# A routed expert kernel: a table of the first 32 tiles, built in eleven pieces beside attention, and a re-ordered turn to the experts

## The reference

```python
x = x + tanh(g_xattn) * attention(layernorm(x), ctx, ctx)
z = layernorm(x)
logits = tanh(z @ Wg1.T) @ Wg2.T
top_logits, top_idx = top_k(logits, 2)
scores = zeros.at[rows, top_idx].set(softmax(top_logits))
up   = einsum('td,ehd->teh', z, Wup) + bup        # 8 experts, 256 wide
down = einsum('teh,eoh->teo', silu(up), Wdown) + bdown
x = x + tanh(g_ffn) * einsum('te,teo->to', scores, down)
```

## Time and profile before

| | us |
|---|---|
| profiled execution, whole | 730.69 |
| its span (first to last instruction) | 728.7 |
| median of three runs | 727.93 |
| PE busy | 639.2 (88%) |
| DVE busy | 520.3 (71%) |
| ACT busy | 381.5 (52%) |
| POOL busy | 356.5 (49%) |

### The profile page before, as it was taken

One profiled execution on the slowest core, in us unless ns is written; L12 is line 12 of the kernel. 1 busy time (PEld: TensorE's weight loads), 2 busy tenths in 40 slices (PEclk: granted clock), 3 DMA queues, 4 the chain that ended last, 5 costly groups with the idle time before them and its releaser, 6 DMA issues.

```text
span 728.7 us, 17222 instructions
## 1 busy us (share of the span) xinstructions
PE 639.2 (88%) x5064; PEld 433.0 (59%) x5064; DVE 520.3 (71%) x1451; ACT 381.5 (52%) x696; POOL 356.5 (49%) x545
## 2 busy tenths in 40 slices
PE   3879999999999999999979884799999989899940
PEld 2445555555555555555534473688989878788930
DVE  3478888888888888888846572466767767787751
ACT  2267777776767676777646431233334434444421
POOL 4122555555555454555553546750031555555755
PEclk9999999999999999999989998799999999999985
DMA  3223444444444444443313674245565899999995
GB/s 99 65 70 103 134 139 136 150 141 143 146 139 142 133 137 136 148 152 121 140 67 133 229 250 172 86 143 163 203 201 182 287 330 297 312 343 326 316 310 178
DMA packets 65027, 129.34 MB, mean 177 GB/s; under 512 B 8640, under 2 KB 12736, under 8 KB 64704
## 3 DMA queue, kind: packets, MB, share of 16 engines
q1 hardware_dynamic: 44496, 77.35, 31.7%
q0 software_dynamic: 10368, 33.56, 14.0%
q10 hardware_dynamic: 10096, 17.59, 7.5%
HBM read 74.20 MB, written 54.26 MB: 176 GB/s over the span
## 4 chain that ended last, share of the span: by engine, by line
PE 67%; DVE 13%; issue 9%; POOL 6%; DVEq 1%; DMA 1%; POOLq 1%; ACT 1%; ACTq 0%
PE s_ps L1196 12%; PE bank_a L1175 8%; DVE nmax L968 7%; PE st_ps L1219 7%; PE st_ps L1317 4%; PE st_ps L1319 4%; PE st_ps L1318 4%; PE s_ps L1300 3%; PE bank_b L1184 3%; PE bank_c L1136 2%; PE bank_q L1327 2%; PE st_ps L1227 2%; PE bank_q L1271 2%; PE bank_q L1328 2%; PE bank_q L1329 2%
## 5 line engine op out<-in xcount | busy, mean ns | idle before, releaser
L968 DVE TENSOR_REDUCE nmax<-s_ps 128x8 f32<-128x1024 f32 x128 | 156.4, 1222 | 65.3 <-PE s_ps L1196 64.4
L1196 PE MATMUL s_ps<-k_t,q_t 32*128 32x256 f32 x1024 | 153.2, 418 | 17.4 <-DVE nmax L968 14.0
L747 ACT ACTIVATE probs<-st_ps 128x1024 f32<-128x1024 f32 x128 | 131.2, 1025 | 69.3 <-PE st_ps L1227 65.8
L1219 PE MATMUL st_ps<-q_t,k_t 32*128 32x512 f32 x512 | 146.8, 650 | 0.3
L1196 PEld LDWEIGHTS s_ps<-k_t,q_t 32*128 32x128 f32 x1024 | 93.0, 193 | 70.0 <-DVE nmax L968 47.8
L690 POOL DMA_INDIRECT y<-expert_out,rows_all x64 | 64.6, 1009 | 66.3 <-DMA expert_out<-y_sb 51.6
L1317 PE MATMUL st_ps<-w_hi,zh 128*128 x284 | 86.4, 304 | 0.9 <-DVE zl L1065 0.9
L819 ACT ACTIVATE t_sb<-u_sb 128x256 f32<-128x256 f32 x71 | 29.7, 418 | 109.2 <-DVE u_sb L1073 92.1
L1319 PE MATMUL st_ps<-w_hi,zl 128*128 x284 | 80.3, 283 | 0.0
L1318 PE MATMUL st_ps<-w_lo,zh 128*128 x284 | 80.1, 282 | 0.0
L700 POOL TENSOR_TENSOR r_in<-r_in,y 128x512 f32<-128x512 f32 x32 | 41.7, 1304 | 64.5 <-DVE y L1094 62.4
(11 more groups left out here) (188 smaller groups left out, 1395.8 us busy)
## 6 DMA issues: line engine op xcount, KB each, us to landing
expert_out<-y_sb SPq DMA_DIRECT2D x71, 256.0 KB, 3.7
z_s<-slots ACTq DMA_DIRECT2D x67, 256.0 KB, 3.5
x_in<-in_x SPq DMA_DIRECT2D x32, 256.0 KB, 2.7
wst<-in_w SPq DMA_DIRECT2D x32, 256.0 KB, 2.6
x_res<-in_x SPq DMA_DIRECT2D x32, 256.0 KB, 2.9
x_scratch<-x_res SPq DMA_DIRECT2D x32, 256.0 KB, 2.0
r_in<-x_scratch SPq DMA_DIRECT2D x32, 256.0 KB, 5.4
out<-r_in SPq DMA_DIRECT2D x32, 256.0 KB, 4.8
```

The source lines that it names most:

```text
L747: a.activation(out, st_ps[:, :].rearrange("t (k n) -> t k n", k=2), ACT.Exp, scale=HD ** -0.5).then_inc(exp_done[half], 1)
L968: v.tensor_reduce(out, s_ps[:, :].rearrange("s (r g c t) -> s r g c t", r=2, g=2, c=2), X_AXIS, ALU.max, negate=True).then_inc(max_done, 1)
L1196: last = t_.matmul(s_ps[:, HALF * rr + 2 * P * gg:HALF * rr + 2 * P * (gg + 1)], q_t[r2][row:row + ROWS32, P * g_:P * (g_ + 1)], k_t[r2][r ...
L1219: t_.matmul(st_ps[:, HALF * rr:HALF * (rr + 1)], k_t[r][row:row + ROWS32, P * i:P * (i + 1)], q_t[r][row:row + ROWS32, :], start=True, sto ...
```

## The change

- The levels become 8, 10, .. 32. A first table covers 32 tiles (`MIDDLE`) from five levels (6 rows of 8 entries, 48 columns), where it covered 11 from one. `EARLY`, the first tile that needs the last scatters and the pads, becomes 9.
- That table is built in eleven pieces, one in each POOL step from 24 to 34, behind `x_res` and ahead of `ve_o`. The loop ends at step 24 instead of 28. The second table runs in the same eleven pieces behind the last scatter.
- ACT waits for the second table at tile 32, and for the four scatter semaphores and the pads at tile 9. `scatter_over` and the `drain` are gone.
- `ends` is written by VectorE instead of POOL; SP reads its eight values with one load and issues the eight pads in one tile step instead of two.
- VectorE reads the expert numbers of four tiles at a time, one tile step earlier in program order, ahead of the mixing instead of behind it.
- The turn is written out anew on VectorE, PE and ACT.
- The last four batches (`LATE` = 28) are mixed by VectorE with two operations each; ACT's scale and POOL's add fall away for them.

```diff
-SEG = (9, 11, 13, 15, 17, 19, 21, 23, 25, 27, 29, 31, 32)
+SEG = tuple(range(8, B + 1, 2))
+KNOWN = 5
+SURE = (KNOWN + 1) * E
+MIDDLE = 2 * SEG[KNOWN - 1]
+PARTS = ((0, MIDDLE), (MIDDLE, TILES))
+LATE = B - 4
-TAB0 = 29
+TAB0 = 24
-LOOP1 = 28
+LOOP1 = 24
-LOADS = 8
+LOADS = 4
...
# SyncE
-                if 5 <= s < 7:
-                    for e in range(4 * (s - 5), 4 * (s - 5) + 4):
-                        pad(e)
+                    _, found = nc.values_load_multi_w_load_instructions(
+                        ends[0:1, :], engines=[mybir.EngineType.SP], min_val=0, max_val=ROWS - P,
...
+                    for row in found:
+                        sp.dma_start(slots_d[bass.ds(row, P), :], r_in[0][:, :]).then_inc(pads_done, 16)
...
# GpSimd, in step(s, u), behind x_res
+                    if isinstance(s, int) and TAB0 <= s < TAB0 + 11:
+                        if s == TAB0:
+                            pool.wait_ge(run_done, SEG[KNOWN - 1])
+                        table(0, s - TAB0)
...
-                if isinstance(s, int) and TAB0 <= s < TAB0 + 3:
-                    first_table(2 * (s - TAB0))
-                    first_table(2 * (s - TAB0) + 1)
...
             pool.wait_ge(run_done, B)
-            g.tensor_copy(ends[:, :], filled[:, B * E:(B + 1) * E]).then_inc(ends_done, 1)
+            for n in range(11):
+                table(1, n)
...
-            ends_at = last_table()
-            for q in range(RING):
-                pool.wait_ge(scattered[q], ring4(B - RING + q, q, 32))
-            pool.drain().then_inc(scatter_over, 1)
...
# ScalarE, tile_rows(t), n = t + RING
+                    if n == MIDDLE:
+                        act.wait_ge(tab_in[1], 32)
+                    if n == EARLY:
+                        scattered_all(act)
+                        act.wait_ge(pads_done, 16 * E)
...
# VectorE
+            def mixed_late(m):
+
+                i, y, r = m - LATE, m % YRING, m % RRING
+                dve.wait_ge(r_loaded[r], 16 * (m // RRING + 1))
+                dve.wait_ge(y2_loaded[y], 16 * (m // YRING + 1))
+                v.scalar_tensor_tensor(r_in[r][:, :], y2[y][:, :], coef[1][:, m:m + 1], r_in[r][:, :],
+                                       ALU.mult, ALU.add).then_inc(late_half, 1)
+                dve.wait_ge(late_half, i + 1)
+                dve.wait_ge(y1_loaded[y], 16 * (m // YRING + 1))
+                v.scalar_tensor_tensor(r_in[r][:, :], y1[y][:, :], coef[0][:, m:m + 1], r_in[r][:, :],
+                                       ALU.mult, ALU.add).then_inc(late_done, 1)
```

More of the change, by code:

```diff
@@ L211, in block_kernel @@
         z = [sb(f"z{i}", [P, D], F32, p1) for i in range(RING)]
+        cap = sb("cap", [P, GROUPS], F32, p1)
+        row0 = sb("row0", [P, GROUPS], F32, p1)
+        drop = sb("drop", [P, GROUPS], F32, p1)
+        scan = [sb(f"scan{i}", [P, PAD + GROUPS], F32, p1) for i in range(2)]
+        over = sb("over", [P, 2 * PAD], F32, p1)
         p1.close()
@@ new lines, in _ @@
+            rows_rest(0)
+            dve.wait_ge(o_rs, b + 1)
+            v.tensor_scalar(z[b % RING][:, :], x_res[p][:, :], mv_o[:, 0:1], rs_o[:, :], ALU.subtract,
+                            ALU.mult).then_inc(z_done, 1)
+            slots_out(b - 2, (b - 2) % RING)
+            rows_rest(1)
+            dve.wait_ge(lg_copied, b)
+            highest(b - 1, 1 - p)
+            biased(0)
+            choices(b - 1, 1 - p)
+            gated(0)
+            choices_out(b - 1)
+            masks(b - 1, 1 - p)
@@ new lines, in up @@
+            def up(t):
+                p = t % 2
+                pe.wait_ge(zl_done, t + 1)
+                o = bank[2 + p][:, 0:HE]
+                for c in range(DC):
+                    cols = bass.ds(expert[t] * (DC * HE) + c * HE, HE)
+                    t_.matmul(o, zh[p][:, P * c:P * c + P], w_hi[:, cols], start=(c == 0), stop=False)
+                    t_.matmul(o, zh[p][:, P * c:P * c + P], w_lo[:, cols], start=False, stop=False)
+                    last = t_.matmul(o, zl[p][:, P * c:P * c + P], w_hi[:, cols], start=False, stop=(c == DC - 1))
+                last.then_inc(up_done, 1)
@@ new lines, in down @@
+            def down(t):
+                p = t % 2
+                pe.wait_ge(hl_done, t + 1)
+                o = bank[4 + p][:, :]
+                for c in range(HC):
+                    cols = bass.ds(expert[t] * (HC * D) + (DOWN0 + c * D), D)
+                    t_.matmul(o, hh[p][:, P * c:P * c + P], w_hi[:, cols], start=(c == 0), stop=False)
+                    t_.matmul(o, hh[p][:, P * c:P * c + P], w_lo[:, cols], start=False, stop=False)
+                    last = t_.matmul(o, hl[p][:, P * c:P * c + P], w_hi[:, cols], start=False, stop=(c == HC - 1))
+                last.then_inc(dn_done, 1)
```

532 lines of the change are left out of this document (283 added, 249 removed).

## The result

| | before | changed |
|---|---|---|
| median of the runs, us | 728.07 (727.07 to 733.02, 4 runs) | 695.93 (695.52 to 697.71, 4 runs) |
| profiled execution, whole | 730.69 | 695.72 |
| its span | 728.7 | 693.9 |
| mean granted clock | 0.967 | 0.978 |

The ratio is 0.9541, 95% interval 0.9504 to 0.9577: 32 us less. The forecast was 701 us (690 to 711); its terms add up to 28 us. The profiled execution of the kernel before was 2.6 us above its median, which is why the two spans differ by more than the medians. I read the spans stage by stage: at five events that both traces have, I take the difference of their times, and what a stage gained is how much that difference grew. Of the 34.8 us between the spans, 1.3 were there before step 29: 0.65 in the first 45 us, and 0.65 from there on, nearly all of it in steps 23 and 24, where the loop of the changed kernel ends.

What follows compares the result with a forecast made beforehand. TensorE sets the pace, busy 88% of the span; its standstills and the tail were counted. Terms 8.5 + 2 + 8 + 4.5 + 5 = 28 us took the profiled 730.69 to 702.7, 699.9 by the median; forecast 701 us, range 690 to 711.

Steps and rivals of the forecast that it cites:

- The first table: Attention around step 32: building GpSimd's table in eleven pieces ends TensorE's wait and slow clock, gaining 8.5 us (6.5 to 9.5).
- The shorter loop: Attention: costed at nothing, because loop steps and written-out steps have the same length.
- The cover behind the residual add: Attention steps: table pieces of 1.0 to 1.8 us hide where GpSimd waits 1.91 us for `mv_o` anyway.
- The turn: From attention to tiles: TensorE's 1.77 us wait for the first gated tile goes, gaining 2 us (0 to 3).
- The gate: ScalarE's wait at tile 9 for scatters and pads: delay 8 us instead of 16, gaining 8 us (2 to 11).
- Rival A: Gate: it moves and hardly shrinks, pads held until 447 us, gain 2 us instead of 8; 707 us, chance 0.15.
- Expert numbers: Tile phase: VectorE reading four at a time costs 4 us instead of 8.4, gaining 4.5 us (0 to 8).
- loads cost by the value: VectorE's expert-number loads: 2.17 us for eight in a quiet stretch, 4.36 under full DMA load, 1.30 for four.
- Rivals B and E: Expert-number loads: B, they give nothing, 705.5 us, chance 0.08; E, doubled load instructions make it slower, 755 us, chance 0.03.
- The tail: After the last tile's store: VectorE mixes the last four batches, so the span ends 5 us earlier (3 to 7).
- The term for the gathers: Tail: without adds between the last pairs of gathers, the last gather ends at about 714 instead of 718.4 us.
- Rival C: Mixing phase: bound by DMA, so the loads' gain and 2 us of the tail are lost; 707 us, chance 0.06.

## Why the prediction was right, and where it was not

- **The first table: right.** Forecast 8.5, measured 8.9; put alone into the kernel before, it brought 12 us in the medians and 8.8 in those steps of the trace. The shorter loop, which I had costed at nothing, is another 0.65 in both; the rest I can't place. The cover behind the residual add, which I had as the ground, was not needed in these steps.
- **The turn: wrong, by its sign.** "VectorE now does `zl` of tile 1 and the bias of tile 0 ahead of the routing chain, so the 1.77 us go; the rest of the work is the same." The wait did go. The rest was not the same: TensorE's two loads of expert numbers had moved ahead of the first transposes, where it has nothing else to do. With the transposes ahead of them the turn took 3.6 us less: 1.3 of gaps and 2.4 behind them, where the lower clock had been. It was then 2.0 us shorter than before, as forecast. In a third trace with that order the clock fell all the same, and 0.5 us were left of the 2.0. I costed the wait that the edit removes, and not what TensorE's new order puts in its place.
- **The gate: right.** Delay 8.5 for a forecast 8, term 8.9 for 8. Two errors cancelled: the pads were down at about 435 us, six earlier than I had it (441.3), but tile 9's load was due seven earlier as well (427.0 for 433.7). The term is right in part by luck. Rival A (a delay of 14) did not happen.
- **Expert numbers: right in sign, wrong in mechanism.** The step "loads cost by the value" failed. I had three rows, 8, 8 and 4 values, all starting at an odd tile, and made a rule of them. The load of eight at tile 0 was in the same trace, with half of the time of the quicker one, and spoke against it:

```profile
L1051 DVEq TENSOR_LOAD <-tab_e x1: 1086/1086/1086, 418.4 to 418.4; - x1
```

  The start decides: moving it in the kernel before brought 7.7 us of the 8.4, and loads of eight in the change are as good as of four. Rivals B and E took their prices from the same slow rows and fall with them.
- **The tiles, what is left.** Of the 9.9 us, 8.2 are the loads, by the trace of the kernel before with moved starts. The median tile also takes 3.45 instead of 3.49 us, which is 2.5 us over 62 tiles; the sum leaves room for 1.7. All ten kernels with the change have 3.45, all four without it 3.49; the cause stays open, and was not tried.
- **The tail: under-sized.** The term for the gathers was 4.4 us. Counted from the last tanh, the last gather ends 4.2 us earlier than in the kernel before; against the changed kernel mixed the old way it starts 4.45 us earlier, 3.9 from the last tanh. What was missing is GpSimd's closing: 5.5 us behind the last operation became 2.5, which is 3.0 of the 7.4 us, and against the changed kernel mixed the old way 6.5 became 2.5. No row before showed it as work, but the span and the last row did: 5.5 us with nothing in them but a store of 2.
- **Rival C** (mixing bound by transfers) did not show in the change, where the tiles kept their pace. It may show in the three kernels whose TensorE is done 7.7 to 11 us earlier: their tails are 5 to 6 us longer.

In the sum the forecast fell 7 us short of the spans: tiles and loads 5.4, tail 2.4, the first steps 1.3, table and gate 1.3, less 3.6 in the turn. That it holds in time is in part luck: of its five terms the turn failed one way and the loads, with a wrong mechanism, the other.

## What to carry to other kernels

Read an odd duration against the operand's address before making a price per element of it. Where an engine reads a table in groups, try starts at multiples of the group: here they took a load of eight from 2.2 to 0.6 us. When one engine's order is rewritten, list what its queue does in the gap that the edit opens, register loads too, and look at the clock behind it. See that GpSimd isn't the last to work: here that was 3 to 4 us. And where transfers are full, don't count on time won by the compute beside them: 11 us of TensorE were 4.9 at the end.

## What was not expected of the hardware

- A register load of eight values: 0.60 us from a multiple of eight, 2.1 to 4.4 us from tile 11, 19 and so on.
- The end of the span lies 5.5 to 6.8 us behind GpSimd's last operation where that is the last of all, 2.5 or 2.6 us behind VectorE's where VectorE is last. The drain inside the kernel before took 6.14 us; without it the distance at the end was 6.8 instead of 5.5, and 6.5 in the two changed kernels that end with GpSimd, so a part of what the drain takes seems to be paid there when it is left out.
- Two gaps of TensorE of 1.46 and 1.25 us, with transposes of 1.09 us between, were followed by the lower clock: 0.87, 0.50 and 0.78 in the three stretches of 4 us from 404 us. With gaps of 0.23 and 1.05, and of 0.25 and 1.04 us, it stayed at 1.00; with gaps of 0.30 and 0.99 us it fell to 0.58 in one such stretch.
